# A fused four-layer kernel: the last layer's feed-forward weights kept exactly ternary, its inputs split in two float32r halves

## The reference, cut to what matters

```python
def _ternary(w):                                   # L3 feed-forward weights
    scale = jnp.maximum(jnp.mean(jnp.abs(w)), 1e-08)
    w_t = jnp.clip(jnp.round(w / scale), -1.0, 1.0)
    return w + jax.lax.stop_gradient(w_t - w)
h = jnp.einsum('bsd,fd->bsf', x, _ternary(W1)) + b1      # 128 -> 512
h = jax.nn.gelu(h, approximate=False)
out = jnp.einsum('bsf,df->bsd', h, _ternary(W2)) + b2    # 512 -> 128
```

## Time and profile before

| | |
|---|---|
| Median of three runs | 1955.6 us (1954.66 to 1956.27) |
| Profiled execution: its own time, its span | 1957.46 us, 1955.7 us |
| Busy in the span: TensorE, VectorE, ScalarE, POOL | 1781.2, 989.1, 843.1, 238.6 us |
| Norm stage before the last layer | 1576.06 to 1594.4 us of the span |
| Last layer: first turn and weights | 1594.7 to 1625.3 us |
| Seven turns of the loop | the first 43.2 us, the others 40.4 us each |
| Last turn | 1911 to 1949 us |
| Mean granted TensorE clock | 0.956 of full |

### The profile page before, as it was taken

The page is one execution under the profiler, slowest core; times in us unless marked ns, Lnnn a source line. Parts: engine busy times, 40 slices in busy tenths (PEclk is TensorE's granted clock), DMA queues, the critical chain, the costliest instruction groups (busy, mean ns, idle before and its releaser), DMA issues. The chain is left out here.

```text
span 1955.7 us, 22682 instructions
## 1 busy us (share of the span) xinstructions
PE 1781.2 (91%) x8518; PEld 1002.1 (51%) x8518; DVE 989.1 (51%) x1612; ACT 843.1 (43%) x1025; POOL 238.6 (12%) x210
## 2 busy tenths in 40 slices
PE   7589999998788989999999999999999979999995
PEld 4222222224453436766767586758576734444442
DVE  3454444444774434444444443434444446677765
ACT  4467777775333324333333243333333343444441
POOL 1000000000561001010101010000001022233322
PEclk8699999998879989999999999999999989999998
DMA  1232222122006620000000000000000010000001
GB/s 71 38 52 44 44 44 44 44 44 113 1 1 141 148 59 0 1 1 1 1 1 1 1 1 1 1 1 1 1 1 0 2 52 1 0 0 0 0 0 43
DMA packets 19116, 48.90 MB, mean 25 GB/s; under 512 B 784, under 2 KB 1552, under 8 KB 18000
## 3 DMA queue, kind: packets, MB, share of 16 engines
q1 hardware_dynamic: 19024, 47.63, 10.0%
HBM read 45.14 MB, written 2.36 MB: 24 GB/s over the span
## 5 line engine op out<-in xcount | busy, mean ns | idle before, releaser
L494 ACT ACTIVATE probs<-ps_ring 128x1024 f32<-128x1024 f32 x256 | 246.0, 1023 | 124.2 <-PE ps_ring L708 121.5
L1733 PEld LDWEIGHTS ps_o<-v,probs 128*128 128x128 f32 x2048 | 236.5, 192 | 34.7 <-issue 31.4
L1733 PE MATMUL ps_o<-v,probs 128*128 128x129 f32 x2048 | 250.8, 279 | 1.8 <-ACT probs L1476 1.2
L1476 ACT ACTIVATE probs<-ps_ring 128x1024 f32<-128x1024 f32 x128 | 127.0, 1024 | 242.1 <-PE ps_ring L1714 242.0
L1546 DVE TENSOR_REDUCE negmax<-ps_o 128x2 f32<-128x1024 f32 x64 | 78.5, 1226 | 167.0 <-PE ps_o L1689 167.0
L722 PE MATMUL ps_o<-probs,v 128*32 128x512 f32 x1024 | 139.3, 618 | 13.1 <-DVE o_sb L545 13.1
L1468 ACT ACTIVATE probs<-ps_ring,pack 128x512 f32<-128x512 f32 x64 | 40.5, 685 | 180.9 <-PE ps_ring L1662 105.5
L1662 PE MATMUL ps_ring<-probs,pack 128*128 128x512 f32 x256 | 117.2, 602 | 0.0
L1559 DVE RECIPROCAL rden<-ps_o 128x2 f32<-128x2 f32 x128 | 21.5, 168 | 178.7 <-PE ps_o L1733 178.7
L1926 POOL TENSOR_TENSOR rs<-r,state 128x512 f32<-128x512 f32 x64 | 81.6, 1275 | 206.6 <-DVE state L2018 202.9
L708 PEld LDWEIGHTS ps_ring<-q_stack,k_stack 32*128 32x128 f32 x512 | 31.6, 187 | 124.9 <-issue 100.6
(11 more groups left out here) (363 smaller groups left out, 3304.9 us busy)
## 6 DMA issues: line engine op xcount, KB each, us to landing
cwb<-combine_by_expert SPq DMA_DIRECT2D x8, 2048.0 KB
score<-score_by_expert SPq DMA_DIRECT2D x7, 2048.0 KB, 13.8
pack<-pack_dram SPq DMA_DIRECT2D x1, 2560.0 KB, 13.3
pack<-pack_dram SPq DMA_DIRECT2D x1, 2443.0 KB, 9.4
x<-x_in SPq DMA_DIRECT2D x2, 1024.0 KB, 6.2
out<-x SPq DMA_DIRECT2D x1, 2048.0 KB, 6.3
score<-score_by_expert SPq DMA_DIRECT2D x1, 1536.0 KB, 13.5
pack<-pack_dram SPq DMA_DIRECT2D x1, 1451.0 KB, 7.6
```

The source lines that it names most:

```text
L494: nc.scalar.activation(probs[n % 3][:, 2 * half:2 * half + 2, :], ps, ACT.Exp, scale=float(HD0) ** -0.5).then_inc(read, 1)
L1476: nc.scalar.activation(probs[:, n % 2, m, :, :], ps, ACT.Exp).then_inc(read, 1)
L1733: last = nc.tensor.matmul(ps_o[:, i, k * (D + 1):(k + 1) * (D + 1)], probs[:, (b * PAIRS + p) % 2, m, j, queries], v[:, m, h, :], start=(m ...
```

## The change

Five edits, all for the last layer:

1. The norm stage becomes `norm_and_split`: behind its own work ScalarE writes `xn_high`, the float32r rounding of `xn`, for eight batches, and POOL writes `xn_low = xn - xn_high` for eight batches.
2. `ternary_weight` ends with one subtraction of two comparisons: exactly -1, 0 or 1, into `tern`. Two tensor_tensor operations and their drains go, on VectorE and on POOL.
3. `up(t)`: one float32 product becomes two float32r passes (low and high half of xn). `down(t)`: likewise, with the two halves of the gelu.
4. ScalarE, behind each gelu: a drain and a copy that writes `hid_high`.
5. POOL, behind `rs(4)` and behind `rs(7)`: two subtractions each, `hid_low = hid - hid_high`. `down(t)` waits for them.

```diff
@@ norm_and_split (was norm_only)
+        @block.gpsimd
+        def _(pool):
+            for b in range(B):
+                pool.wait_ge(high_ready, b + 1)
+                nc.gpsimd.tensor_tensor(single(xl[:, at(b)]), xn[:, at(b)], xh[:, at(b)], ALU.subtract).then_inc(low_ready, 1)
+            pool.wait_ge(low_ready, B)
...
             ln_act(act)
+            for b in range(B):
+                act.wait_ge(normed, b + 1)
+                nc.scalar.activation(single(xh[:, at(b)]), xn[:, at(b)], ACT.Copy).then_inc(high_ready, 1)
@@ ternary_weight
-            nc_engine.tensor_scalar(mag[n][:, :], m, bound[:, 4 + n:5 + n], None, ALU.is_lt)
-            nc_engine.tensor_scalar(tern[n][:, :], m, bound[:, 2 + n:3 + n], None, ALU.is_gt)
+            nc_engine.tensor_scalar(hid[:, 2 * n, :], m, bound[:, 4 + n:5 + n], None, ALU.is_lt)
+            nc_engine.tensor_scalar(hid[:, 2 * n + 1, :], m, bound[:, 2 + n:3 + n], None, ALU.is_gt)
             eng.drain()
-            nc_engine.tensor_tensor(tern[n][:, :], tern[n][:, :], mag[n][:, :], ALU.subtract)
-            eng.drain()
-            nc_engine.tensor_tensor(tern[n][:, :], tern[n][:, :], m, ALU.subtract)
-            eng.drain()
-            nc_engine.tensor_tensor(m, m, tern[n][:, :], ALU.add).then_inc(ternary[n], 1)
+            nc_engine.tensor_tensor(single(tern[n][:, :]), hid[:, 2 * n + 1, :], hid[:, 2 * n, :], ALU.subtract).then_inc(ternary[n], 1)
@@ POOL, in the loop over j, behind rs(j)
+                        if j in (4, 7):
+                            for t in range(2 * (j // 7), 2 * (j // 7) + 2):
+                                pool.drain()
+                                pool.wait_ge(gelued, b * FT + t + 2)
+                                nc.gpsimd.tensor_tensor(single(hid_low[:, t, :]), hid[:, t, :], hid_high[:, t, :], ALU.subtract
+                                                        ).then_inc(hid_low_ready, 1)
@@ ScalarE, gelu(t)
-                    nc.scalar.activation(hid[:, t, :], ps_f[:, t % 2, :], ACT.Gelu, bias=w["b1_3"][:, t:t + 1]).then_inc(gelued, 1)
+                    act.wait_ge(hid_low_ready, b * FT + 1)
+                    nc.scalar.activation(hid[:, t, :], ps_f[:, t % 2, :], ACT.Gelu, bias=w["b1_3"][:, t:t + 1])
+                    act.drain()
+                    nc.scalar.activation(single(hid_high[:, t, :]), hid[:, t, :], ACT.Copy).then_inc(gelued, 1)
@@ TensorE, up(t) and down(t)
-                    nc.tensor.matmul(ps_f[:, t % 2, :], w["W1_3"][:, t * P:(t + 1) * P], xn[:, at(b)], start=True, stop=True).then_inc(up_done, 1)
+                    w1 = single(tern[0][:, t * P:(t + 1) * P])
+                    nc.tensor.matmul(ps_f[:, t % 2, :], w1, single(xn_low[:, at(b)]), start=True, stop=False)
+                    nc.tensor.matmul(ps_f[:, t % 2, :], w1, single(xn_high[:, at(b)]), start=False, stop=True).then_inc(up_done, 1)
...
-                    nc.tensor.matmul(ps_x[:, :], w["W2_3"][:, t * P:(t + 1) * P], hid[:, t, :], start=(t == 0), stop=False)
+                    nc.tensor.matmul(ps_x[:, :], w2, single(hid_high[:, t, :]), start=(t == 0), stop=False)
+                    pe.wait_ge(hid_low_ready, b * FT + t + 2)
+                    nc.tensor.matmul(ps_x[:, :], w2, single(hid_low[:, t, :]), start=False, stop=False)
```

More of the change, by code:

```diff
@@ L1254, in _, with norm_and_split @@
                     unproject(b)
-def norm_only(nc, sh, name, load=None):
+def norm_and_split(nc, sh, name, load):
+    xn, xh, xl = sh["xn"], sh["xn_high"], sh["xn_low"]
     with ExitStack() as ctx:
@@ L1261, in norm_only @@
         ps = ctx.enter_context(nc.psum_tensor(f"{name}_ps", [P, 8, 512], F32))
-        ln_pe, ln_dve, ln_act, _ = layer_norm(nc, ctx, sh, xc, ps)
+        high_ready, low_ready = (ctx.enter_context(nc.semaphore(f"{name}_{n}")) for n in ("high_ready", "low_ready"))
+        ln_pe, ln_dve, ln_act, normed = layer_norm(nc, ctx, sh, xc, ps)
         block = ctx.enter_context(nc.Block())
@@ L1266, in _ @@
         def _(sp):
-            if load is not None:
-                sp.dma_start(sh["w"][load].tensor[:, :], sh["w_dram"][load]).then_inc(sh["w_loaded"][load], 16)
+            sp.dma_start(sh["w"][load].tensor[:, :], sh["w_dram"][load]).then_inc(sh["w_loaded"][load], 16)
+        @block.gpsimd
[4 more added lines that the diff above has]
+            pool.wait_ge(low_ready, B)
         @block.tensor
@@ L1847, in layer3_mix @@
         y, yc, sq, rstd, o = (sb(f"{n}3", [P, T]) for n in ("y", "yc", "sq", "rstd", "o"))
-        hid = sb("hid3", [P, FT, T])
+        hid, hid_high, hid_low = (sb(f"{n}3", [P, FT, T]) for n in ("hid", "hid_high", "hid_low"))
+        xn_high, xn_low = sh["xn_high"], sh["xn_low"]
         mag, tern = ([sb(f"{name}3_{n}", [P, FF]) for n in range(2)] for name in ("mag", "tern"))
@@ L1873, in layer3_mix @@
         squared, rstd_ready, o_ready = sem("squared3"), sem("rstd_ready3"), sem("o_ready3")
-        up_done, gelued = sem("up_done3"), sem("gelued3")
+        up_done, gelued, hid_low_ready = sem("up_done3"), sem("gelued3"), sem("hid_low_ready3")
         out_done, x_added = sem("out_done3"), sem("x_added3")
@@ L1938, in _ @@
             act.sem_inc(gelued, 1)
+            act.sem_inc(hid_low_ready, 1)
             def turn_program(turn):
@@ L2152, in down @@
                         pe.wait_ge(x_added, b)
+                    w2 = single(tern[1][:, t * P:(t + 1) * P])
                     pe.wait_ge(gelued, b * FT + t + 2)
-                    nc.tensor.matmul(ps_x[:, :], w["W2_3"][:, t * P:(t + 1) * P], hid[:, t, :], start=(t == 0), stop=False)
+                    nc.tensor.matmul(ps_x[:, :], w2, single(hid_high[:, t, :]), start=(t == 0), stop=False)
+                    pe.wait_ge(hid_low_ready, b * FT + t + 2)
+                    nc.tensor.matmul(ps_x[:, :], w2, single(hid_low[:, t, :]), start=False, stop=False)
                 value(0)
@@ L2258, in program @@
             sh["w"][4] = pack(ctx, 5)
-            norm_only(nc, sh, "norm3", 4)
+            for part in ("high", "low"):
+                sh["xn_" + part] = sb(ctx, "xn_" + part, [P, NTOK])
+            norm_and_split(nc, sh, "norm3", 4)
             layer3_mix(nc, sh)
```

## The result

The changed kernel takes 1969.3 us in the median (1966.92 to 1971.37, four runs), the kernel before 1955.93 beside it: a ratio of 1.0067, 95% interval 1.0049 to 1.0084, so 9.6 to 16.4 us slower. 1968 was forecast. The profiled executions give spans of 1967.5 and 1955.7 us.

A forecast was written before the change was run, and what follows sets the result against it. TensorE paces the turn on average, but behind the mean of y a chain sets the time, and VectorE and POOL block each other. 10.0 - 1.5 + 1.4 + 2.6 = +12.5 us, giving 1968 us, range 1957 to 1973.

The forecast's parts named there:

- Norm stage, +10.0: End of the norm stage: POOL's eight subtractions of 1.27 us lie open, nothing of the last layer covers them; +10.0 us.
- Ternary weights, -1.5: Ahead of the first loop turn: two tensor_tensor operations go, TensorE's pause becomes 2.6 us, the clock still falls; -1.5 us.
- the bound of the prediction: First loop turn: possible gain if the clock did not fall in the pause ahead of it, not counted; 2.8 us.
- Passes: TensorE in each turn: two float32r passes replace a float32 product, saving 1.56 us for up and 1.56 for down.
- the downs' half: Behind the mean of y: down's 1.56 us saving is lost, since the chain there sets the time.
- The 0.1 us at var: Behind the mean of y: with downs 0 and 1 shorter, var moves ahead only to the square's end, 0.1 us.
- the prediction's chain of square, var and Ln: Behind the mean of y: mean, yc, square, var, Ln, Exp and o set the time, TensorE's products only fill it.
- POOL's subtractions, +0.2 a turn: Each loop turn: POOL's hid_low and VectorE's scans hold each other up, eating up's 1.56 us; +0.2 us a turn.
- Last turn, +2.6: Last turn: hid_low alternates with scans, TensorE idles, then runs at half clock; +2.6 us, ends 0 and 4.
- POOL slipping in: Rival, 0.15: POOL's operation starts at once beside a running scan, each turn gains 1.56 us; 1953 us.
- The dearer handover, +0.8 a turn: Rival, 0.15: POOL gets in only at VectorE's full end, scan 6 precedes the second hid_low; +0.8 a turn, 1972 us.
- TensorE pacing all: Rival, 0.04: the chain behind the mean of y shrinks with its products, a turn gains 3.1 us; 1945 us.

The follow-up runs named there:

- e1: Kernel before with only the split of xn added to the norm stage, both halves written and not read: 1967.4 us, ratio 1.0056 to the kernel before.
- e2: Changed kernel with down in float32 again, without ScalarE's gelu copies and POOL's four subtractions a turn: 1954.1 us, ratio 0.9991 to the kernel before.
- e3: Changed kernel with POOL's four subtractions a turn replaced by memsets that read nothing, down's second pass rereading the high half: 1957.7 us, ratio 1.0011 to before.
- e4: Changed kernel with down as one float32 product, ScalarE's copies, POOL's subtractions and the wait for them kept: 1968.7 us, ratio 1.0069 to the kernel before.
- v2: As v1, plus float32r down, POOL's four subtractions behind the halves of xv and all downs behind g: 1945.3 us, ratio 0.9943 to the kernel before.
- e5: Changed kernel with all four of POOL's gelu subtractions behind rs(7), none behind rs(4): 1955.0 us, ratio 0.9993 to the kernel before.
- v1: Changed kernel with down in float32, no gelu split, and xn's split moved from the norm stage into the turns: 1942.6 us, ratio 0.9932 to before.
- v3: As v1, with three unused float32 products filling TensorE's pause ahead of the first loop turn: 1941.7 us, ratio 0.9935 to the kernel before.

## Why the prediction was right, point by point

- **Norm stage, +10.0.** Measured +9.9 in the changed kernel and in e1. POOL's start-to-start step was 1.23 us, with no drain between the operations, for the 1.27 taken. That nothing covers it was the step that decided the sign, and e1 shows it alone.
- **Ternary weights, -1.5.** The pause went from 4.15 to 2.64 us. Another 0.5 us of that stage's -2.0 lies ahead of the pause and is no effect of the change: from the first cast to the gate at the pause it is 25.8 to 26.5 us in all ten profiles, with or without the split, and shorter where the clock came back sooner behind the cast (10.9 us behind it in the changed kernel, 11.8 before). The clock fell, as expected, but that was in part luck: at the same pause it fell for half as long in e2, e3, e4 and v2 and not at all in e5 and v1. With no fall the turn would have been some 2.8 us shorter, the bound of the prediction (an estimate: it is 3.1 us above the other turns, and 0.3 above them in e5 and v1).
- **Passes.** Ups 0.46 us apart, as forecast. That the downs' half is lost stands in e4 (+0.02 us a turn) and v2 (0.0). The 0.1 us at var came out as 0.05 and was worth nothing even so: the prediction's chain of square, var and Ln had the wrong link in it, ScalarE's table load stands where it had var (v2).
- **POOL's subtractions, +0.2 a turn.** The mechanism was right operation by operation: the first `hid_low` 2.21 us long, scan 6 at 2.31, pick 5 waiting (1.16 us idle where 1.4 was forecast), `rs(6)` ahead of scan 7, pick 7 0.20 us later. The size was short: 0.36 a turn. The missing 0.16 lies behind pick 7, where no term was set down: `u` starts 0.96 us behind pick 7, which had waited, and not 0.86, and the mean of y then meets `y` (1.09 us recorded for 1.02). These two make 0.10 and 0.07 us. Scans of 1.7 to 2.3 us were forecast, 2.31 and 2.32 came. POOL gets the reads about 0.2 us ahead of the scan's recorded end; 0.1 had been taken from rows 8.
- **Last turn, +2.6.** Measured +1.5. Two `hid_low` and `rs(5)` alternated with the scans (2.00, 1.99 and 1.92 us on POOL), TensorE stood 4.61 us, and it went on at half clock, as forecast. kv 3, which waits for TensorE, is in the lines too:

```profile
1929.17 0.69 DVE L2033 TENSOR_TENSOR kv<-k,ps_ring 128x512 f32<-128x512 f32 x1 [0.83 <-PE ps_ring L1340]
...
1935.31 2.00 POOL L1938 TENSOR_TENSOR hid_low<-hid,hid_high 128x512 fp32r<-128x512 f32 x1 [0.16 <-issue]
...
1937.46 1.99 POOL L1938 TENSOR_TENSOR hid_low<-hid,hid_high 128x512 fp32r<-128x512 f32 x1 [0.16 <-issue]
...
1941.64 2.08 PE L2145 MATMUL ps_y<-rs,pack 128*128 128x512 f32 x2 [4.61 <-POOL rs L1933]
...
1947.43 1.02 PE L2128 MATMUL ps_ring<-ruk,pack 128*128 128x512 f32 x2
```

  The forecast had worked out +3.2 and took 2.6. Two of its terms are mis-sized, both by the clock. The larger: pick 5 stands 21.0 us behind `ruk`, not 22.0 (1932.3 less 1910.26, `ruk` before). The scans run 2.2 us ahead of before at kv 3 (8.54 us behind `ruk` for 10.78), not 1.5. TensorE's first pick still ran at full clock, which fell 0.8 us behind its start, at 1925.72, for 3.4 us only; before, it had fallen 0.8 us ahead of that pick, at 1913.72, for 6.8. In e4 it fell inside the pause ahead of that pick, for 6.8, and there kv 3 is 1.4 us ahead of before and pick 5 at 21.8, close to the forecast. The smaller: six us of work at half clock were taken behind pick 5, and the clock was back about 4.6 us after pick 5 began (0.90 in the window from 1946 to 1947), so `u` stands 5.8 us behind pick 5, where the forecast had 6.4 (its four terms add up to 6.5). Rows 10 had been read from the pick on; counted from the fall, the low stretch is 6.8 us there and here, and here 2.3 us of it had run before pick 5.
- **The sum.** +11.9 us between the profiles for +12.5 is closer than its terms, and that is luck: the seven loop turns came out 1.5 us dearer than forecast (0.5 of it in the first, where the clock has a part), and the last turn 1.1 us and the stage ahead of the loop 0.5 us cheaper. The executions themselves differ by several us (1951.3 to 1964.0 over all runs of the kernel before).
- **The rivals.** POOL slipping in is ruled out by 2.21 and 1.90 us on POOL. The dearer handover, +0.8 a turn, is ruled out too: the second `hid_low` went ahead of scan 6. The rule of the Trainium skill (page "SBUF — State Buffer", section "Who interferes with whom") holds in kind, also in that POOL operations which only write do not contend with the scans (e3), but for "the whole instruction" these records show 0.2 us less, and that decided who came next. TensorE pacing all is ruled out by e4.
- That the kernel could be kept within the uncertainty by placing the same work elsewhere was not seen: e5 alone, two subtractions moved, is worth 1.4 us in each of seven turns, 10 us.

## What to carry to other kernels

Work on an idle engine is free only if it ends ahead of what the others wait for and leaves alone what they share: here ten us lay open because a block waits for all its engines, and four idle-looking operations cost 1.66 us a turn, 1.4 of it because two of them stood ahead of three others that TensorE needed, on reads that VectorE's scans needed. The same operations showed no cost a few us later (v2), in a gap that the timeline of before already showed (15 us ahead of the first `rs`). And before passes are made cheaper, see in the chain which half of them it waits for: of 3.1 us a turn 1.3 were to be had.

## What the runs showed of the hardware

**The clock.** In every profile TensorE pauses ahead of the first loop turn. By the windows of one us, the granted clock did this there:

| Kernel | Pause | Clock fell, behind the pause's start | At half clock for | First loop turn over the others |
|---|---|---|---|---|
| before | 4.15 | 2.45 | 6.8 | 2.8 |
| changed | 2.64 | 1.98 | 6.8 | 3.1 |
| e1 | 4.15 | 5.3 | 3.4 | 2.0 |
| e2, e3, e4, v2 | 2.61 to 2.64 | 2.4 to 2.55 | 3.4 | 1.6 to 1.9 |
| e5, v1 | 2.60, 2.61 | no fall | 0 | 0.3 |
| v3 | filled | no fall | 0 | 0.3 |

v1's windows:

```profile
1621.00:1622.00 1.00, 0.00 (x0) 0.00 (x0) 0.93 (x3) 0.22 (x1) 0.00 (x0) 1.00 0.00 0
1622.00:1623.00 1.00, 0.33 (x1) 0.30 (x2) 1.00 (x3) 0.00 (x0) 0.00 (x0) 1.00 0.00 0
```

So the length of a pause of this size does not settle whether the clock falls. Where it fell here and in the last turns ahead of `u`, it was low for either 3.4 or 6.8 us, and that alone moves the first loop turn by up to 3 us between profiles. The last turn shows the same. Ahead of its first pick TensorE pauses for 3.0 us in all kernels. In e4 the clock fell inside that pause, for 6.8 us; in the changed kernel it fell 3.8 us behind the pause's start, for 3.4. Both have a second stretch of 6.8 us, which ended 5.6 us behind pick 5 in e4 and 4.6 in the changed kernel. That makes e4's last turn longer by 0.8 us up to pick 5 and by 0.5 from there to `u`, which is its whole 1.3 us. What decides between 3.4, 6.8 and no fall is left open.

**VectorE and POOL.** The CAST of `xv_high`, with one input and one output in SBUF, takes 0.43 us with POOL idle, as the trace of the kernel before has it (L2051). It takes 1.33 us beside a subtraction on POOL, and 1.04 us beside a memset in e3, which reads nothing. So this cast, other than a scan (1.28 us beside a memset), is held by a POOL operation that only writes as well.
